# Slot table of a routed layer: hot rows on Pool, constant matmuls ahead of the products, FFN matrices loaded one by one

## The reference: what is computed

```python
logits = jnp.einsum('bsd,de->bse', input, Wg)
top_vals, top_idx = jax.lax.top_k(jax.nn.softmax(logits, axis=-1), 2)
...
h = jax.nn.relu(jnp.einsum('ebsd,edh->ebsh', xm, W1) + b1[:, None, None, :])
y = jnp.einsum('ebsh,ehd->ebsd', h, W2) + b2[:, None, None, :]
```

## Time and profile before

| | |
|---|---|
| median of 3 runs | 2008.87 us (2008.82 to 2013.36) |
| the profiled execution, its own time | 2003.96 us |
| its span, first to last instruction | 2002.3 us |
| mean granted PE clock | 0.872 of full |
| busy: PE, DVE, ACT, POOL | 83%, 64%, 41%, 11% |

### The profile page before, as it was taken

One profiled execution on the slowest core, in us unless ns is written; L12 is line 12 of the kernel. 1 busy time (PEld: TensorE's weight loads), 2 busy tenths in 40 slices (PEclk: granted clock), 3 DMA queues, 4 the chain that ended last, 5 costly groups with the idle time before them and its releaser, 6 DMA issues.

```text
span 2002.3 us, 25995 instructions
## 1 busy us (share of the span) xinstructions
PE 1658.1 (83%) x7870; PEld 945.4 (47%) x7870; DVE 1273.5 (64%) x2524; ACT 823.4 (41%) x1231; POOL 218.7 (11%) x287
## 2 busy tenths in 40 slices
PE   6858999992899987759999694899996958999686
PEld 2657888881433334524333363433333624333354
DVE  3772232202689929748995696598928847897386
ACT  1302333321277652134777222266752233677421
POOL 0002222203000002100000030010001200001000
PEclk8958999995699998866999796789987966999888
DMA  3127777762312001022210020312001113220000
GB/s 115 64 67 225 233 226 231 228 183 69 64 29 39 2 1 48 17 52 34 40 27 2 0 64 22 63 20 38 11 1 32 32 33 54 33 33 2 0 1 21
DMA packets 86062, 122.93 MB, mean 61 GB/s; under 512 B 16458, under 2 KB 62668, under 8 KB 85916
## 3 DMA queue, kind: packets, MB, share of 16 engines
q1 hardware_dynamic: 73916, 97.79, 19.0%
q0 software_dynamic: 12000, 23.35, 4.1%
HBM read 76.71 MB, written 18.61 MB: 48 GB/s over the span
## 4 chain that ended last, share of the span: by engine, by line
PE 66%; DVE 20%; issue 6%; ACT 3%; DMA 2%; SPq 1%; POOL 1%; DVEq 0%; ACTq 0%; POOLq 0%
PE PS L824 12%; PE PS L867 11%; DVE MX L1274 8%; PE PS L942 7%; PE PS L749 7%; PE PS L761 7%; PE PS L952 4%; PE PS L810 3%; PE PS L854 2%; PE PS L802 2%; PE PS L909 1%; DVE st L1221 1%; PE PS L728 1%; SPq L420 1%; PE PS L969 1%
## 5 line engine op out<-in xcount | busy, mean ns | idle before, releaser
L1274 DVE TENSOR_REDUCE MX<-PS 128x1 f32<-128x512 f32 x1024 | 637.2, 682 | 96.1 <-PE PS L824 95.2
L606 ACT ACTIVATE Pb<-PS 128x1024 f32<-128x1024 f32 x512 | 498.1, 1023 | 213.7 <-PE PS L854 213.0
L824 PE MATMUL PS<-Ks,Qs 48*128 48x512 f32 x1024 | 392.8, 503 | 46.1 <-DMA Ks<-OT 20.5
L824 PEld LDWEIGHTS PS<-Ks,Qs 48*128 48x128 f32 x1024 | 176.1, 207 | 365.9 <-DVE MX L1274 325.2
L854 PE MATMUL PS<-Qs,Ks 50*128 50x512 f32 x1024 | 313.1, 457 | 10.8 <-ACT Pb L606 5.9
L867 PE MATMUL PS<-Pb,V 128*32 128x512 f32 x2048 | 285.8, 631 | 2.8 <-ACT Pb L606 2.8
L854 PEld LDWEIGHTS PS<-Qs,Ks 50*128 50x128 f32 x1024 | 149.5, 196 | 63.8 <-ACT Pb L606 53.2
L1203 DVE TENSOR_TENSOR V<-PS,V 128x512 f32<-128x512 f32 x39 | 27.0, 691 | 217.4 <-PE PS L761 217.4
L476 POOL DMA_DIRECT2D Qs<-MR x128 | 65.0, 515 | 793.4 <-DVE MR L1287 302.4
L761 PE MATMUL PS<-Pb,OT 128*128 128x256 f32 x624 | 141.0, 379 | 0.0
L541 ACT ACTIVATE OT<-PS,b1t 128x256 f32<-128x256 f32 x156 | 65.4, 470 | 158.2 <-PE PS L749 158.2
(11 more groups left out here) (252 smaller groups left out, 1916.0 us busy)
## 6 DMA issues: line engine op xcount, KB each, us to landing
Pb<-W SPq DMA_DIRECT2D x78, 512.0 KB, 3.8
y_slot<-V SPq DMA_DIRECT2D x39, 256.0 KB, 3.7
Qs<-Qh SPq DMA_DIRECT2D x128, 64.0 KB, 2.4
Ks<-Kh SPq DMA_DIRECT2D x128, 64.0 KB, 2.4
V<-b SPq DMA_DIRECT2D x39, 128.0 KB, 3.4
V<-x_mid POOLq DMA_DIRECT2D x4, 1024.0 KB, 6.4
out<-X SPq DMA_DIRECT2D x4, 1024.0 KB, 4.9
OT<-xT SPq DMA_DIRECT2D x2, 1024.0 KB, 6.6
```

What stands on the lines that cost most here:

```text
L606: F["ex"].inc(act.activation(Pb[:, kt % 2, 2 * qh:2 * qh + 2, :], PS[:, 2 * qh:2 * qh + 2, :], ACT.Exp, scale=0.25))
L824: F["slp"].inc(pe.matmul(PS[:, slot_bank(i), :], Qs[rows, p % NB, t * P:(t + 1) * P], Ks[rows, p % NB, kh * HALF:(kh + 1) * HALF], start=T ...
L1274: F["sld"].inc(dve.tensor_reduce(MX[:, p % 2, a, t, kh:kh + 1], PS[:, slot_bank(i), :], AX.X, ALU.max))
```

## The change

Three parts. First, `low_hot` of sequences 0 and 1 leaves DVE; POOL runs the same 32 instructions as soon as `place(0)` has written `low` (a new counter `lw` releases it, a new counter `lh` tells PE). DVE writes `high_hot(1)` earlier, right behind the table of tiles. Second, PE runs 14 matmuls of constants (`warm(14, 2)`: identity times 512 columns of `wqkv`, into a bank nobody reads) between `ranks(1)` and the products; the wait for `s_late` moves from behind the products to ahead of `state_out(0)`, since `wqkv` is now read earlier. Third, the three FFN matrices get a semaphore each, and SP issues them at tiles 1, 4 and 7, behind the store of y, in place of all three at tile 0; DVE waits for each before it quantizes it.

```diff
@@ sync
-                if k == 0:
+                if k >= 2:
+                    store_y(k - 2)
+                if k in (1, 4, 7):
                     for q in range(2):
                         C[f"mid{q}"].wait(sp, 16 * B // 2)
-                    for w, src in enumerate((w_gate, w_up, w_down)):
-                        load_ffn(w, src)
-                if k >= 2:
-                    store_y(k - 2)
+                    load_ffn(k // 3, (w_gate, w_up, w_down)[k // 3])
@@ gpsimd
+            C["lw"].wait(pool, 1)
+            for b in range(2):
+                for k in range(2):
+                    for t in range(TT):
+                        ins = pool.tensor_scalar(lowhot[b][:, k * TT + t, :], lane[:, :], low[:, b, k, t:t + 1],
+                                                 token[:, b * TT + t:b * TT + t + 1], ALU.is_equal, ALU.mult)
+            C["lh"].inc(ins)
@@ tensor
+            def warm(n, bank):
+
+                for _ in range(n):
+                    ins = pe.matmul(PS[:, bank, :], ident[:, :], wqkv[:, 0, 0:HALF], start=True, stop=True)
+
+            pe.wait_ge(s_late, N_LATE)
             for h in range(2 * B):
...
             ranks(1)
+            warm(14, 2)
+            C["lh"].wait(pe, 1)
             for b in range(B):
...
             C["ix"].inc(ins)
-            pe.wait_ge(s_late, N_LATE)
@@ vector
+                if g == 0:
+                    dve.sem_inc(C["lw"].sem, 1)
+                    C["lw"].seen += 1
...
             norm(5)
-            low_hot(0)
             norm(6)
...
-            for b in range(1, B):
+            high_hot(1)
+            for b in range(2, B):
                 low_hot(b)
                 high_hot(b)
...
             def weight_quant():
-                dve.wait_ge(s_wld, 16 * 3)
                 for w in range(3):
+                    dve.wait_ge(s_wld[w], 16)
```

More of the change, by code:

```diff
@@ L238, in transformer @@
         s_wq = sem("s_wq")
-        s_wld = sem("s_wld")
+        s_wld = [sem(f"s_wld{w}") for w in range(3)]
         s_late = sem("s_late")
@@ L351, in load_ffn @@
             def load_ffn(w, src):
-                sp.dma_start(WN[w], src.rearrange("(t p) k -> p t k", p=WP if w < 2 else P)).then_inc(s_wld, 16)
+                sp.dma_start(WN[w], src.rearrange("(t p) k -> p t k", p=WP if w < 2 else P)).then_inc(s_wld[w], 16)
             for b in range(B):
```

## The result

The changed kernel takes 1979.57 us in the median of 4 runs (1973.62 to 1981.68). The kernel before, run beside it, takes 2008.93 us. The ratio is 0.984, 95% interval 0.9818 to 0.9863: 29 us faster. The profiled execution took 1979.27 us.

The account below looks back on a forecast made before the run. The prediction took DVE to bound the kernel before 113 us, then PE's half-clock products, then a slow gather. Gains of 9.8 and 6.0 us made 15.8, so 2008.87 - 15.8 = 1993.1 us, range 1987 to 2003.

Parts of the forecast that it names:

- the gather: Tile 0's second gather lands in 4.0 us with FFN matrices later; PE's first expert turn gains 6.0 us.
- the sum: Whole kernel: 9.8 us from the slot table plus 6.0 from the gather, 15.8 us, carried unchanged to the end.
- POOL's instructions: POOL's 32 one-hot instructions: 0.45 us each, done before 100 us; cover of 1.05 us each.
- DVE's shift of 0.9 us: Everything to the end of `high_hot(0)` comes 0.9 us earlier: 2.2 gained less 1.3 lost beside POOL.
- the 2.2: Gain to the end of `high_hot(0)` from removing 32 DVE instructions: last statistics at 94.5 in place of 96.71 us.
- whole instructions waited out: Upper bound of DVE's loss beside POOL: 12 two-input instructions each wait a whole POOL instruction, 5.4 us.
- the stated ends: Bounds on DVE's net shift before the products: 2.2 and -3.2 us.
- Constants: Before the products, 14 constant matmuls raise PE's clock after 5.3 us; they last about 14.6 us.
- the rival: The constants never raise the clock; products end at 155.6 us, total 2016 us; 4 in 100.
- Products: Slot table's products at full clock: 0.11 us apart, 3.5 us a sequence, ending at 132.6 us, 9.8 us gained.
- The clock falls during the products: Rival: sequences 2 and 3 of the slot table run at half clock; 9.0 us gained, 1999.9 us; 18 in 100.
- Late matrices cost nothing: In the expert stage, FFN matrices issued later delay nothing; without cover each would cost 3 us, 9 in all.

Follow-up runs that it names:

- e5: The kernel before plus 14 matmuls of 8x8 (56 instructions) while PE waits for its first input; ratio 0.9865.
- e13: The kernel before plus 64 matmuls of 8x8 (256 instructions, one whole 16 KB block) while PE waits for its first input; ratio 1.001.
- e6: The changed kernel plus 50 matmuls of 8x8 while PE waits; with the constants 256 added instructions, one whole block; ratio 0.9895 to the kernel before.
- e7: The changed kernel with its 14 constant matmuls replaced by 14 of 8x8 while PE waits for its first input; ratio 0.9889 to the kernel before.
- e4: The changed kernel without its 14 constant matmuls; ratio 0.9939 to the kernel before.
- e8: The changed kernel with DVE writing all one-hot rows in its old order, without POOL's part; ratio 0.9849 to the kernel before.
- e12: The changed kernel with 7 constant matmuls in place of 14, plus 7 of 8x8 while PE waits; ratio 0.9895 to the kernel before.
- e3: The kernel before with POOL's rows and the constants, but all three FFN matrices still loaded at tile 0; ratio 0.9898.
- e1: The kernel before, unchanged, for a second profile; ratio 1.001.
- e9: The changed kernel again, unchanged, for a second profile; ratio 0.9842 to the kernel before.
- e14: The kernel before plus 3 matmuls of 8x8 (12 instructions) while PE waits for its first input; ratio 0.9999.

## Why the prediction was wrong

The mechanism of the table and of the gather was right; the failed step is the last sentence of the sum, "From the expert stage on the work is PE's and unchanged, so the shift is carried to the end". The work was unchanged, the place of its code was not. e5 puts the price of this alone at 27 us in the kernel before (ratio 0.9865), and e13 takes it back. With the change in, the same comparison gives less: 11 us for a whole block (e6 against the changed kernel), 10 us for the 56 instructions (e7 against e4).

1. **POOL's instructions: right that they are in time, mis-sized.** The groups of POOL by form:

```profile
L439 POOL TENSOR_SCALAR OT<-lane,low,token 128x128 f32<-128x128 f32 x32 | 25.6, 812 | 81.9 <-DVEq L1093 81.9
```

0.80 us each on the timeline (25.58/32) against 0.45 forecast and a limit of 1.05. They end at 109.3, PE asks at 119.2.

2. **DVE's shift of 0.9 us: wrong in sign.** `high_hot(0)` starts 0.7 us later than in the earlier trace rows. The last statistics end at 96.0, not 94.5: in the rows of half sequence 7 PE ran at half clock for a while (the row of 90.31 us, four instructions in 1.97 where 1.05 is the full-clock length), behind a wait of 2.10 us for ACT. So 0.7 us came of the 2.2. The rest is DVE beside POOL. One instruction, after, and in e8 without POOL:

```profile
99.50 0.45 DVE L1065 TENSOR_TENSOR rt<-rt,rev_sb 128x128 f32<-128x128 f32 x1
```

```profile
99.36 0.29 DVE L1057 TENSOR_TENSOR rt<-rt,rev_sb 128x128 f32<-128x128 f32 x1
```

Such instructions grew by up to 0.17 us, not by POOL's 0.80, and some with one input grew too (a copy of 16 elements from 0.18 to 0.40). From the last statistics to `high_hot(0)` DVE is busy 15.3 us where before and e8 have 13.9: 1.4 us lost, against 1.3 forecast, far from the 5.4 of whole instructions waited out. So the mis-sized term is the 2.2 us. The net of -0.7 us lies inside the stated ends.

3. **Constants: right.** 14.52 us against 14.6, with 5.3 us of them at half clock assumed; the clock rose at 109.5, after 4.7. The argument against the rival, "every dense stretch of the trace rose within 6.2 us", was a wrong reading: the products of the earlier trace rows are dense for 27.7 us at 0.50, and so is the stretch from 516.70 us above.

4. **Products: right.** 0.111 us apart at 1.00 against 0.11; they start 0.6 us later than forecast, and `idx` comes 8.8 us earlier against 9.8. "The clock falls during the products" did not happen, but e8 and e12 show how near it is: there it fell behind waits of 1.8 and 2.1 us. (The bound for products of 0.14 us was added up wrongly: 128 x 0.03 is 3.8 us less, not 5.9.)

5. **The gather: right, and better.** From the second gather's issue to the first turn 2.93 us against 4.0. e3 confirms the cause: with the matrices at tile 0 the wait is 12.95 us.

6. **Late matrices cost nothing: not quite.** From the first turn to the last second layer the kernels with the matrices at tile 0 take 294.7 to 295.6 us, those with late ones 296.2 to 299.0. In the changed kernel 1.4 of the 16.0 us are lost by the end of the stage, 0.8 of them by tile 3, mostly in tile 0's first layer at half clock (6.61 against 5.84 us). `w_gate` was used 12.9 us after its issue, not some 5, and PE lost nothing to that.

So 14.6 us at the end of the expert stage against 15.8. The rest, 10.2 us in the profiles, is a gain and a loss. From the last projection to the last value projection the four sequences take 93.4 us in place of 115.4: 22 us gained, as in e5 (93.6), by the place of the code. From the last score to the last product of the FFN (called the FFN stage here) they take 499.0 us in place of 488.8: 10 us lost. Other stages differ by 1.4 us at most.

This loss goes with the session and not with the kernel. The FFN stages sum to 487.7 to 491.0 us in the profiles of before and e1 to e8, and to 496.1 to 499.9 in those of after and e9 to e14, although e13 and e14 hold no part of the change and e3, e7 and e8 hold some. The kernel before, timed beside them, had medians of 1998.7 and 2003.3 us in the short sessions and 2008.0 to 2010.8 in the long. In the long ones ACT waits once or twice more in the FFN stage of sequences 0 to 2 before it reads PE's result, 6.83 us in e14 (at 801.46) where before has 3.82 at that place, and the page's chain has a share for "another core or an unknown queue" that the short ones lack. What sets it stays open; no profile of before fell in a long session.

Shown by the pads is that the place of the code makes the loop longer or shorter. That it does so by the packet that delays the transfers, and by the longer wait ahead of the half clock, is shown as a coincidence in every sequence of every kernel; by which resource the packet delays them was not measured.

## What to carry to other kernels

Before a gain or a loss far from an edit is explained by the edit, look where the instruction queue's packets fall against the short transfers that an engine waits for, and pad by a part of a block and by a whole block to see what layout alone is worth. Here it was worth 1.35% in the kernel before and 0.5% in the changed one, where all three parts together brought 14.6 us, 0.7%, up to the loop. Take both profiles in one session, too: a stage that no edit touched differed by 10 us between sessions. Warm the clock with constants only if they last until the data come: half of them brought `idx` 0.5 us (141.77 against e4's 142.22).

## What was unexpected in the hardware

- With a single 16 KB packet of the instruction queue beside them, 64 KB transfers landed 0.8 us later (3.1 for 2.3 us), the wait was 1.3 us longer (5.40 for 4.10), and the stretch behind it 6 to 7 us, in which PE ran at 0.50 for up to 24 us although it was busy throughout (23.80 of 23.80 us).
- Products of 78 columns kept a clock of 1.00 for 14.5 us once they had it, never raised it from 0.50 in 27.7 us, and lost it behind waits of 1.8 and 2.1 us.
- POOL took 0.80 us for a two-operation instruction of 128x128, and DVE's instructions with two inputs grew from 0.29 to at most 0.45 us beside it, a small copy from 0.18 to 0.40.
- Medians of one unchanged kernel went from 1998.7 to 2010.8 us between chips and sessions, 0.6%, more than some parts of the change bring; one chip had 2003.3 in one session and 2008.0 in another.
